# Layer 1's values four units at a time, the next image's statistics in its heads, and a one-source column of maxima

## What is computed

```python
x = x + L0(_gn(x), ...)      # _gn: group norm, 32 groups, over tokens and the group's channels
x = x + L1(_gn(x), ...)
# L0: full attention, 12 heads of 64, softmax(q k / 8 + rel_h + rel_w) v, then Wp
# L1: 7 x 7 neighbourhood attention, 12 heads of 64, then out_w
```

## Time and profile before

| | us |
|---|---|
| median of three runs | 3282.05 |
| the profiled execution | 3277.68 |
| its span, first to last instruction | 3275.9 |
| TensorE busy | 3157.8 (96%) |
| VectorE busy | 1758.0 (54%) |
| ScalarE busy | 1229.8 (38%) |
| GpSimd busy | 1079.4 (33%) |
| mean granted TensorE clock | 0.996 of full |

### The profile page before, as it was taken

The page is one execution under the profiler, slowest core; times in us unless marked ns, Lnnn a source line. Parts: engine busy times, 40 slices in busy tenths (PEclk is TensorE's granted clock), DMA queues, the critical chain, the costliest instruction groups (busy, mean ns, idle before and its releaser), DMA issues.

```text
span 3275.9 us, 48913 instructions
## 1 busy us (share of the span) xinstructions
PE 3157.8 (96%) x20428; PEld 2355.6 (72%) x20428; DVE 1758.0 (54%) x1889; ACT 1229.8 (38%) x1397; POOL 1079.4 (33%) x618
## 2 busy tenths in 40 slices
PE   8999999999999999999999999999999999999999
PEld 6875558886787555888678755588777875568876
DVE  4447745446445874544644578444464458844444
ACT  2345542133334554213333455321333355532142
POOL 0037760024004776003400477500330047750043
PEclk9999999999999999999999999999999999999999
DMA  3211013104321001311432100121043111022113
GB/s 123 93 33 24 20 48 113 39 30 151 98 92 31 20 19 48 113 39 36 149 110 75 33 20 17 59 103 48 27 160 109 65 36 24 13 82 87 39 33 113
DMA packets 167928, 210.95 MB, mean 64 GB/s; under 512 B 113568, under 2 KB 126112, under 8 KB 167712
## 3 DMA queue, kind: packets, MB, share of 16 engines
q1 hardware_dynamic: 166176, 206.25, 20.1%
q10 hardware_dynamic: 1536, 1.57, 0.2%
HBM read 132.26 MB, written 50.33 MB: 56 GB/s over the span
## 4 chain that ended last, share of the span: by engine, by line
PE 77%; DVE 8%; issue 5%; ACT 4%; SPq 3%; DMA 2%; POOL 0%; ACTq 0%; DVEq 0%; POOLq 0%
PE score L1113 15%; PE score L1114 13%; PE score L1115 13%; PE lot L1269 10%; PE score L1234 8%; PE lot L1184 5%; PE lot L1187 3%; SPq L420 3%; PE score L1241 2%; PE score L1247 2%; DVE recip L897 2%; DVE b_lo L889 1%; DMA recip<-recip 1%; PE lot L1155 1%; PE lot L1286 1%
## 5 line engine op out<-in xcount | busy, mean ns | idle before, releaser
L538 POOL TENSOR_TENSOR acc<-acc,prob 128x1024 f32<-128x1024 f32 x288 | 704.7, 2447 | 250.9 <-ACT prob L718 224.9
L718 ACT ACTIVATE prob<-score 128x1024 f32<-128x1024 f32 (+3 forms) x576 | 512.8, 908 | 393.3 <-PE score L1247 321.0
L855 DVE TENSOR_REDUCE max_part<-lot 128x1 f32<-128x512 f32 x640 | 411.1, 684 | 154.0 <-PE lot L1187 154.0
L1269 PE MATMUL lot<-prob,v 128*64 128x512 f32 (+4 forms) x2496 | 470.3, 514 | 10.5 <-ACT o_raw L617 10.5
L1113 PE MATMUL score<-a_hi,w_hi 128*128 128x512 f32 x1152 | 459.2, 399 | 18.0 <-DVE w_lo L783 6.2
L1114 PE MATMUL score<-a_lo,w_hi 128*128 128x512 f32 x1152 | 450.7, 391 | 0.0
L1115 PE MATMUL score<-a_hi,w_lo 128*128 128x512 f32 x1152 | 450.0, 391 | 0.0
L538 POOL TENSOR_TENSOR acc<-prob 128x1024 f32<-128x1024 f32 x48 | 113.8, 2370 | 779.0 <-ACT prob L718 779.0
L1113 PE MATMUL score<-w_hi,a_hi 128*128 128x256 f32 x1152 | 336.1, 292 | 0.0
L783 DVE TENSOR_TENSOR w_lo<-raw,w_hi 128x1536 fp32r<-128x1536 f32 x95 | 178.0, 1873 | 294.0 <-ACT w_hi L575 293.4
L1269 PEld LDWEIGHTS lot<-prob,v 128*64 128x64 f32 x2496 | 161.5, 137 | 238.8 <-issue 204.5
(11 more groups left out here) (111 smaller groups left out, 5467.2 us busy)
## 6 DMA issues: line engine op xcount, KB each, us to landing
raw<-weights SPq DMA_DIRECT2D x96, 768.0 KB, 4.4
g_mem<-g SPq DMA_DIRECT2D x24, 1024.0 KB, 4.7
xin<-x_t SPq DMA_DIRECT2D x24, 512.0 KB, 6.5
xr<-x_t SPq DMA_DIRECT2D x24, 512.0 KB, 5.1
x_mem<-xr SPq DMA_DIRECT2D x24, 512.0 KB, 6.8
xr<-x_mem SPq DMA_DIRECT2D x24, 512.0 KB, 6.4
y_t<-xr SPq DMA_DIRECT2D x24, 512.0 KB, 4.5
recip<-recip SPq DMA_DIRECT2D x368, 32.0 KB, 1.8
```

The lines of the kernel that those rows point to most:

```text
L538: nc.gpsimd.tensor_tensor(acc[:, :, a:b], with_, now, ALU.add).then_inc(added, 1)
L718: nc.scalar.activation(prob[:, ug % P_SLOTS, :, 0:b - a], score[:, u % 2, :, 0:b - a], ACT.Exp, scale=SCALE).then_inc(prob_ok, 1)
L855: nc.vector.reduce_max(max_part[:, t, part, h:h + 1], lot[:, (2 * n + h) % 3, :], AX.X)\
L1269: last = nc.tensor.matmul(lot[rows_of(h), bank, x - half * HALF:y - half * HALF], v[:, t, p * 128 + 64 * h:p * 128 + 64 * h + 64], prob[:, ...
```

## The change

**Values.** Layer 1's `values` of units 0 to 3 stand behind unit 5's scores, those of units 4 to 7 behind unit 1 of the next pair (or at the end).

**Statistics.** A buffer `x_next` of three tiles lies over weight slot 1 during layer 1's heads. SP loads the next image's tiles to it, three before the heads, three in pairs 0 and 1; DVE makes their statistics at the end of its part for pairs 0, 1 and 2 and aggregates in pair 3. Chunk 9's load goes to pair 3, and the casts and splits of chunks 9 and 10 go from pairs 0 and 1 to pairs 4 and 5. The group table is loaded in pair 5. The means have a place of their own in bank 1 (`means_at`); `mean_averages` comes before the output, `shift_averages` after its first four products' group. The image is loaded again to `xin` for the norm, and norms and splits are made earlier among the output adds; `norm` waits for that load.

**Maxima.** `columns` is one reduction over `max_part` in place of a maximum of two operands.

**ACT's order in layer 0.** In pairs 1 to 4 `bias_hi` comes before unit 13's exponential, and `bias_first` after it. In layer 1 the output's copy comes one unit later.

The diff, with the smallest edits left out (the signature of `averages`, the place of the means, the source of the statistics) and the indentation cut:

```diff
@@ -265,6 +265,9 @@
+    x_next = m.put("x_next", [128, 3, TOKENS], at=slot_at[1])
@@ -311,6 +314,7 @@
+    next_in = sems("next_in", 3)
@@ -452,13 +460,35 @@
...
         load_bias(f, 2)
-    else:
-        weights(f, 9)
+    def next_tile(i):
+        if f + 1 == PHASES:
+            return
+        if i < 3:
+            sp.wait_ge(v_mm, f * VN + 2 * QT)
+        else:
+            sp.wait_ge(bn_ok, 2 * ((f + 1) * CT + i - 2))
+        sp.dma_start(x_next[:, i % 3, :], x_in[image + 1, :, i, :]).then_inc(next_in[i % 3], 16)
+    if layer == 1:
+        for i in range(3):
+            next_tile(i)
...
         if layer == 1:
+            if p == 3:
+                if f + 1 < PHASES:
+                    sp.wait_ge(bn_ok, 2 * (f + 2) * CT)
+                weights(f, 9)
+            if p == LAST and f + 1 < PHASES:
+                sp.wait_ge(shifted, pair_no(f, LAST))
+                sp.dma_start(group[:, :, :], group_src).then_inc(group_in, 16)
...
                 spread(f, p - 1, 0)
+            if p == 0:
+                next_tile(3)
+                next_tile(4)
+            if p == 1:
+                next_tile(5)
@@ -480,7 +510,7 @@
...
     sp.wait_ge(sum_mm, last_part(f, last))
-    if f + 1 < PHASES:
+    if layer == 0:
@@ -738,17 +768,17 @@
...
                     out_copy(f, p, 0)
-                    if ahead:
-                        bias_first(f, p + 2)
-                if u == 13 and p < LAST:
+                if u == (12 if p else 13) and p < LAST:
                     bias_hi(f, p + 1)
+                if u == 13 and ahead:
+                    bias_first(f, p + 2)
             else:
-                if u == 1 and p:
+                if u == 2 and p:
...
                     sums_copy(f, p - 1, 0)
-                if u == 6 and p < 2:
-                    weight_hi(f, QK_CHUNKS + V_CHUNKS + p)
+                if u == 6 and p >= 4:
+                    weight_hi(f, QK_CHUNKS + V_CHUNKS + p - 4)
@@ -763,13 +793,15 @@
...
     out_hi(f, LAST, last)
-    weight_hi(f, CHUNKS - 1)
...
             input_hi(f + 1, i)
-            if i == 3:
-                weight_hi(f + 1, 0)
-    elif layer == 0:
+            if i == 2:
+                weight_hi(f, CHUNKS - 1)
+        weight_hi(f + 1, 0)
+    else:
+        weight_hi(f, CHUNKS - 1)
+    if layer == 0:
@@ -818,11 +850,13 @@
...
     dve.wait_ge(gshift_ok, norm_no(f, k))
-    nc.vector.scalar_tensor_tensor(variance[:, t], mx[:, 1, t], EPS,
+    nc.vector.scalar_tensor_tensor(variance[:, t], mx[:, 1, 0:CT][:, t], EPS,
...
     dve.wait_ge(rstd_ok, norm_no(f, part_of(f, i)))
+    if f and f % 2 == 0:
+        dve.wait_ge(xin_in[i], 16 * (f // 2 + 1))
@@ -859,8 +893,8 @@
...
 def columns(f, p):
-    nc.vector.tensor_tensor(max_col[:, p, :, :], max_part[:, :, 0, :], max_part[:, :, 1, :],
-                            ALU.max).then_inc(col_ok, 1)
+    nc.vector.reduce_max(max_col[:, p, :, :], max_part[:, :, :, :].rearrange("p t a h -> p t h a"),
+                         AX.X).then_inc(col_ok, 1)
@@ -1009,12 +1043,18 @@
...
                 normalise(f, p - 2, 0)
-            if p < 2:
-                weight_lo(f, QK_CHUNKS + V_CHUNKS + p)
...
                 out_lo(f, p - 2, 0)
+            if p < 3 and nx < PHASES:
+                for i in (2 * p, 2 * p + 1):
+                    dve.wait_ge(next_in[i % 3], 16 * (image * 2 + i // 3 + 1))
+                    statistics(nx, i)
+            if p == 3 and nx < PHASES:
+                aggregate(nx, 0)
+            if p >= 4:
+                weight_lo(f, QK_CHUNKS + V_CHUNKS + p - 4)
@@ -1045,16 +1085,18 @@
...
     else:
+        if nx < PHASES:
+            group_means(nx, 0)
+            group_variances(nx, 0)
...
     if layer == 1 and nx < PHASES:
-        for i in range(CT):
-            dve.wait_ge(xin_in[i], 16 * (image + 2))
-            statistics(nx, i)
-        aggregate(nx, 0)
+        norm(nx, 0)
+        norm(nx, 1)
+        input_lo(nx, 0)
@@ -1066,7 +1108,7 @@
...
             nc.vector.tensor_tensor(dst, out_at(n), dst, ALU.add).then_inc(o_ok, 1)
-        if n == 5:
+        if n == 5 and (layer == 0 or nx == PHASES):
@@ -1092,20 +1134,21 @@
...
         elif nx < PHASES:
+            if n == 5:
+                norm(nx, 2)
+                input_lo(nx, 1)
+                norm(nx, 3)
             if n == 6:
-                group_means(nx, 0)
+                weight_lo(f, CHUNKS - 1)
+                input_lo(nx, 2)
+                norm(nx, 4)
             if n == 7:
-                group_variances(nx, 0)
-            if n >= 7:
-                norm(nx, n - 7)
-            if n >= 8:
-                input_lo(nx, n - 8)
+                input_lo(nx, 3)
+                norm(nx, 5)
+            if n in (8, 9):
+                input_lo(nx, n - 4)
...
                 weight_lo(nx, 0)
-            if n == 11:
-                norm(nx, 5)
-                input_lo(nx, 4)
-                input_lo(nx, 5)
@@ -1130,15 +1172,17 @@
...
     pe.wait_ge(mv_ok, f * CT + norm_parts(f)[k][-1] + 1)
-    if f:
+    if f % 2:
         pe.wait_ge(sums_out, last_part(f - 1, LAST))
-    averages(f, k, 0, mean_var, 2, gsum_ok)
+    elif f:
+        pe.wait_ge(shifted, pair_no(f - 1, LAST))
+    averages(f, k, means_at(f), mean_var, 2, gsum_ok)
...
         pe.wait_ge(var_ok, norm_no(f, k - 1))
-    averages(f, k, 1, shift2[:, 1, :].unsqueeze(2), 1, gshift_ok)
+    averages(f, k, mx[:, 1, :], shift2[:, 1, :].unsqueeze(2), 1, gshift_ok)
@@ -1361,12 +1405,12 @@
...
                 scores(f, p, u)
-                if u % 2 and u > 1:
-                    values(f, p, u - 3)
-                    values(f, p, u - 2)
+                if u == GROUPED + 1:
+                    for e in range(GROUPED):
+                        values(f, p, e)
                 elif u == 1 and p:
-                    values(f, p - 1, QT - 2)
-                    values(f, p - 1, QT - 1)
+                    for e in range(QT - GROUPED, QT):
+                        values(f, p - 1, e)
@@ -1407,10 +1451,15 @@
...
     pe.wait_ge(prob_ok, unit_no(f, last_pair, UNITS[layer] - 1))
+    early = layer == 1 and f + 1 < PHASES
+    if early:
+        mean_averages(f + 1, 0)
...
             output(n, c)
+        if early and c == 0:
+            shift_averages(f + 1, 0)
@@ -1428,10 +1477,10 @@
...
             output(n, c)
-        if f + 1 < PHASES:
-            if n == 6 + (layer == 0):
+        if layer == 0:
+            if n == 7:
                 mean_averages(f + 1, 0)
-            if n == 7 + (layer == 0):
+            if n == 8:
```

15 lines of the change are left out of this document (8 added, 7 removed).

## The result

The changed kernel takes **3256.47 us** (median of four runs, 3255.83 to 3263.17); the kernel before, beside it, 3279.56 (3274.67 to 3285.32). The ratio is 0.9934, 95% interval 0.9912 to 0.9956, 23 us faster. The forecast was 3250, its range 3234 to 3267. The profiled execution of the changed kernel is the slowest of its four (3263.17), so its trace shows 14.5 us less span, not 23.

The account below looks back on a forecast made before the run. TensorE, busy 3157.8 of 3275.9 us, was taken as the bound. Boundary 19.2 + layer 0 16.1 - heads 4.4 = 30.9 us off 3277.7 gives 3246.8, as a median 3251; forecast 3250 us, range 3234 to 3267.

Parts of the forecast that it names:

- Boundary: Three image boundaries: waits on output adds and first weights, restarts and three dips go, less waits for means; net 19.2 us gained.
- wait for the means: Image boundaries: TensorE's second averages wait for VectorE's copies of the means; 1.0 us each, bounds nothing to about 2.8.
- no clock dip there: Sign of being right: at the three boundaries no wait on an output add and no clock dip.
- Layer 0: Pairs 1 to 4 gain by the column and ScalarE's order, pair 0 loses; net 16.1 us gained, bounds 4 and 28.
- two dips, 3.3 us: Layer 0's pair 0: its stall becomes 3.4 us long and brings clock dips in two of four images, 3.3 us in all.
- no cost by bias_first: Layer 0's upper bound: 28 us gained if the late bias_first costs nothing.
- D: Rival, layer 0: the one-source column waits for GpSimd too, 1.0 us in 16 pairs does not come; 3266 us, chance 0.08.
- E: Rival, layer 1's heads: statistics wait for GpSimd adds like two-source operations, kernel slower; 3298 us, chance 0.04.
- Heads: Layer 1's heads: 10.8 us from fewer switches outweighed by waits on exponentials and weight casts; net 4.4 us slower, bounds -12 and +8.
- A: Rival: layer 0 gives only 4 us, unit 13's late exponential and bias_first stall TensorE and bring dips; 3262 us, chance 0.17.
- B: Rival: boundary stall returns as wait for the means, 2.8 us and a 1.6 us dip each; 3260 us, chance 0.12.
- C: Rival, layer 1's heads: drained switches won in full as ScalarE keeps up, +8 instead of -4.4; 3238 us, chance 0.19.

Follow-up runs that it names:

- e8: Changed kernel with ScalarE's pair 0 order as before and the second averages issued after the second four outputs: 3241.1 us, ratio 0.9888.
- e5: Kernel before with one edit, the column of maxima as a one-source reduction: 3247.6 us, ratio 0.9912.
- e4: Changed kernel without layer 0's part and without the grouping of values: 3267.2 us, ratio 0.9969.
- e7: e1 with layer 1's values in twos again: 3242.3 us, ratio 0.9897.
- e2: Kernel before with layer 1's values in fours and the output's copy one unit later: 3286.3 us, ratio 1.0023.
- e1: Changed kernel with ScalarE's order in layer 0's pair 0 as before: 3248.0 us, ratio 0.9909.
- e9: Changed kernel with ScalarE's order in layer 0 as before in all pairs, one-source column kept: 3239.2 us, ratio 0.9878.
- e12: e11 with the weight casts of layer 1's pairs 4 and 5 at unit 5 instead of 6: 3225.5 us, ratio 0.9839.
- e11: e9 with the second averages after the second outputs and layer 1's values in twos: 3220.9 us, ratio 0.9820.
- e3: Kernel before with both layer 0 edits, the one-source column and ScalarE's new order: 3265.8 us, ratio 0.9964.

## Why the prediction was right, and where it was not

The time fell into the range, but the parts did not add up as forecast: the table's rows come to 30.9 us forecast and 15.1 in the traces, and the medians differ by 23.1. That 3256.5 lies within 3234 to 3267 owes something to the width of the range. The kinds of wait were foreseen nearly all, the clock behind them was not.

**Boundary (19.2 forecast, 9.4 measured).** The statistics in the heads cost nothing (670 ns each, none over 682), and the wait on the adds and on the first weights went, and the three dips behind the former: right. The wait for the means was put at 1.0 us and is 1.1: right. Missing was its price: I took three dips away and set none behind the new waits. The sign "no clock dip there" held at one boundary of three. Between pair 4's and pair 5's sums the changed kernel takes 19.32, 20.81 and 22.47 us; the last two have the dips, together 4.6 us. The first has none and is 1.6 longer than e8, which has no wait: 1.7 more than forecast for three. The 2.4 us of the second casts belong to this row too. These three make 8.7 of the 9.8 us that are lacking. The dips are the mis-sized term: they were put at nothing behind the new waits and measured 4.6 us.

**Layer 0 (16.1 forecast, 10.2 measured).** The pairs came out as worked: 1.72 us instead of 1.55 each (1.59 with a single wait of 1.4 us in image 2), and the wait for `bias_first` 0.61 instead of 0.7. In pair 0 the waits cost some 0.6 us an image, near the forecast's 0.8. What was too small is the clock: two dips, 3.3 us, were set there, and all four images have one, two of them twice as long; the row is 10.6 us longer, of which some 8 are clock. (The forecast's sign named a wait of about 2 us there, its working 3.4; it is 3.44.) The +2.3 us of the last pair can't be charged to the change: over all kernels run here that row lies between 175.3 and 180.9 us, with a wait of 2.7 to 4.3 us for an exponential in each image and a dip behind it in 50 of 56. The step that failed most is how the gain was shared out. I gave 1.0 us a pair to the column and 0.55 to the new order, without working out what the column does alone. Alone it is worth 2.38 (e5), and the order is a loss of 0.64 in pairs 1 to 3 and all of pair 0. The upper bound of 28 us "no cost by bias_first" was nearly this case (31.8 in e5's trace), and I took it for out of reach.

The Trainium skill, SBUF — State Buffer, section "SBUF: two separate sides", has VectorE shut out by GpSimd only with two SBUF inputs or in a mode that takes both ports. The trace agrees: the one-source column takes 0.19 us everywhere (186 ns mean of 24, 16 of them wholly within one GpSimd add), and the statistics 0.67 (at most 0.68 in the six that lie wholly within one). So rivals D and E fell.

**Heads (4.4 us slower forecast, 4.6 measured).** That the two agree is luck. Of the 4.4 us only 2.0 belong to the measured stretch, and of the 4.6 some 5.0 are three dips behind pair 4's wait (10.7 us with one and 9.1 without, from pair 5's shift to pair 4's sums), which were in no term. Without them the heads are as long as before: each pair gained 0.22 us (12.45 instead of 12.67; 0.05 to 0.3 forecast), and the 1.26 us at pair 4 (1.2 forecast) took it back. The last values wait 0.4 us (0.6 forecast). The sum also hides that pairs 1 and 2 could have been 12.04 in this kernel, as the statistics took the casts out of them (e4, e7): beside those, the grouping is a loss of 0.4 there.

The Trainium skill, TensorEngine Tiling (Array Packing), "Key Properties", says that a change of tiling mode drains TensorE. No run shows the 10.8 us that I had estimated from the rows for fewer switches: in fours the exponentials set the pace (12.45 us, with and without `out_hi`), and grouping alone is 9 us slower (e2). The drain itself was not measured apart.

**Rivals.** A (layer 0 gives little) was the nearest for the time: layer 0 gave 10 instead of 16, but by its first pair and the clock, not by the exponential of unit 13. B had the right place and the wrong size: 1.1 us, and a dip at two of three boundaries, not 2.8 and a dip at each (its 3260 is 10 us above the forecast, since 1.0 a boundary stood in the sum already). C fell, with pairs at 12.45.

**What stays open.** Which of the waits brings a dip. In the profiled runs the clock fell behind pair 4's 1.26 us wait in three of four images in the changed kernel, in two of four in e1 and in all four in e8 and e9, the work around it being the same; behind waits of the same 1.26 us for an exponential in e2's pairs 0 and 1 it never fell (8 cases). Nor did it behind any of the four 1.26 us waits on `q_lo` that each of the fourteen profiled kernels has in its projections, or behind the 1.69 us of the earlier trace rows. So the length of a wait alone doesn't decide, and no experiment here separates what does. e12 has a dip in image 3's pair 0 that e11 has not, with the same waits there. Open too is a single wait of 1.4 us on DVE's maxima in pair 3 of image 2, in the changed kernel and in e12 only. Missing clock is between 10 and 29 us over these kernels, so up to half of a change of this size can be clock, and one trace does not tell it.

## What to carry to other kernels

Work out each edit of a change alone before sharing a gain between two of them: where one instruction holds a chain of three engines, shortening it may end the waits further down too, and a reordering made for those waits then only costs. A small two-source VectorE operation beside GpSimd adds (16 elements in 1.75 us) is worth rewriting as a one-source one wherever a chain hangs on it. Beside a wait that a change leaves or makes on a full TensorE, write a possible clock dip of some 1.6 us, with a chance of its own: behind 3.44 us there was one in 8 of 8 cases (changed kernel, e3), behind pair 4's 1.26 us in 13 of 16, and behind the 1.26 us waits on `q_lo` in 0 of 56. Moving the wanted work some 2.6 us away from its producer (e8 against e1) won 6.9 us by the medians, where the three waits were 3.3. And compare a grouping at each place of the work that it has to cover: here it may have gone from a loss to a gain with the place of one cast.

## What the runs showed of the hardware

A six-element two-source subtraction on VectorE took 1.32 us beside a GpSimd add and 0.17 us free of one (L843 in e4 and in the changed kernel); it ended 0.02 us after the add in progress, as the 16-element column of the kernel before did (329.65 and 329.61 us). Here the price was what was left of the add, not the size of the operation. One-source reductions and statistics beside the same adds kept 0.19 and 0.67 us. And a clock dip of about 1.65 us came behind PE waits of only 0.7 to 1.3 us (e4, e12, pair 4's end: 10.7 us with one and 9.1 without), not only behind those of 3.3 us that the kernel before shows, but only at some places: none came behind the waits of 1.1 to 1.7 us on `q_lo`, `a_lo` and `w_lo` between the projections' products, in fourteen traces.
